# Four GNN layers on one core: phase ends without an all-engine barrier, and semaphores of finished phases cleared by POOL behind a pass's last gather

## What is computed

```python
edge_index = jnp.stack([src, dst])
x = _layernorm(x + _L0_gnn_ref(x, edge_index, ...), axis=-1)                 # attention, exp of clipped dots
x = _layernorm(x + _L1_gnn_ref(x, edge_index, edge_attr_64, ...), axis=-1)   # messages from x[src] and an edge MLP
x = _layernorm(x + _L2_gnn_ref(x, edge_attr_3, edge_weight, src, dst, ...), axis=-1)  # radial MLP, vectors
x = _layernorm(x + _L3_gnn_ref(x, ..., src, dst), axis=-1)                   # softmax over each node's edges
```

## Time and profile before

| | us |
|---|---|
| median of 3 runs (5058.72 to 5064.53) | 5061.64 |
| the profiled execution | 5061.25 |
| its span | 5059.5 |
| mean granted TensorE clock, share of full speed | 0.86 |
| busy: PE, DVE, ACT, POOL | 3558.8, 3631.7, 2794.9, 3588.2 |

### The profile page before, as it was taken

How to read it: one execution, slowest core, us unless ns; L and a number is a source line. 1 busy time by engine, 2 the same in 40 slices (tenths; PEclk the granted TensorE clock), 3 DMA queues, 4 the chain that set the end, 5 groups by cost and what they waited for, 6 DMA issues and landing times. The chain is left out here.

```text
span 5059.5 us, 96093 instructions
## 1 busy us (share of the span) xinstructions
PE 3558.8 (70%) x20064; PEld 2945.0 (58%) x20065; DVE 3631.7 (72%) x8845; ACT 2794.9 (55%) x7180; POOL 3588.2 (71%) x3861
## 2 busy tenths in 40 slices
PE   5445444542476666666688888888779999999993
PEld 4444444442365555555566666666667777777772
DVE  5666666667654444444787777777679999999998
ACT  2444444444622222222576666666558888888885
POOL 4777777775677777776277777777548877777773
PEclk8777777776687777777789999999899999999997
DMA  6544444442433333332022112122157767766662
GB/s 186 157 156 156 156 156 156 156 156 87 122 84 79 80 80 80 80 80 73 28 68 57 56 56 57 56 56 57 38 147 195 191 189 189 190 188 190 189 190 55
DMA packets 491118, 596.80 MB, mean 118 GB/s; under 512 B 127483, under 2 KB 349165, under 8 KB 490639
## 3 DMA queue, kind: packets, MB, share of 16 engines
q0 software_dynamic: 141696, 349.47, 24.9%
q1 hardware_dynamic: 348463, 245.90, 16.9%
q10 hardware_dynamic: 864, 0.39, 0.1%
HBM read 505.89 MB, written 30.07 MB: 106 GB/s over the span
## 5 line engine op out<-in xcount | busy, mean ns | idle before, releaser
L917 DVE TENSOR_TENSOR acc<-acc,banks 128x256 f32 (+1 forms) x3520 | 1346.2, 382 | 599.8 <-PE banks L893 410.1
L893 PE MATMUL banks<-e_rows,e_sel 128*128 128x256 f32 x3520 | 961.2, 409 | 110.4 <-DVE acc L917 105.1
L832 POOL DMA_INDIRECT e_rows<-fsv_t,e_index x820 | 815.7, 995 | 246.9 <-issue 246.9
L832 POOL DMA_INDIRECT e_rows<-kv_t,e_index x820 | 789.9, 963 | 249.7 <-issue 245.5
L832 POOL DMA_INDIRECT e_rows<-x_t,e_index x820 | 774.7, 945 | 257.1 <-issue 243.2
L832 POOL DMA_INDIRECT e_rows<-up_t,e_index x820 | 774.6, 945 | 249.9 <-issue 207.3
L868 ACT ACTIVATE e_away<-node_iota,local 128x128 f32<-128x128 f32 x2640 | 837.0, 387 | 8.4 <-issue 1.9
L893 PEld LDWEIGHTS banks<-e_rows,e_sel 128*128 128x128 f32 x3520 | 663.4, 204 | 253.2 <-DVE acc L917 166.4
L893 PE MATMUL banks<-e_msg,e_sel 128*128 128x137 f32 (+1 forms) x3520 | 756.8, 364 | 7.4 <-DVE acc L917 3.4
L994 PE MATMUL banks<-acc,e_sel_t 128*128 x1760 | 314.4, 334 | 566.9 <-DVE e_sel_t L961 551.9
L1131 ACT ACTIVATE e_rows<-banks,e_rows 128x128 f32<-128x128 f32 x880 | 251.4, 370 | 775.0 <-PE banks L1122 374.0
(11 more groups left out here) (209 smaller groups left out, 6438.0 us busy)
## 6 DMA issues: line engine op xcount, KB each, us to landing
e_near<-near_d SPq DMA_DIRECT2D x440, 258.0 KB, 4.4
e_far<-acc SPq DMA_DIRECT2D x880, 64.0 KB
e_attr<-in_attr_rows SPq DMA_DIRECT2D x880, 32.0 KB
e_rows<-kv_t,e_index POOLq DMA_INDIRECT x820
e_rows<-x_t,e_index POOLq DMA_INDIRECT x820
e_rows<-up_t,e_index POOLq DMA_INDIRECT x820, 2.5
e_rows<-fsv_t,e_index POOLq DMA_INDIRECT x820
kv_t<-proj_kv SPq DMA_DIRECT2D x12, 512.0 KB
```

Of the source, the lines that this page charges most:

```text
L832: G.indirect_dma_start(out=self.rows[:, u, i, 0:self.width], out_offset=None, in_=self.table, in_offset=bass.IndirectOffsetOnAxis(ap=index ...
L893: m = PE.matmul(bank[n_bank][:, col + at:col + at + rows.shape[1]], self.place_of_sel(g)[:, i, :], rows, start=True, stop=True)
L917: V.tensor_tensor(to, to, bank[n_bank][:, col:col + self.sums].unsqueeze(1), ALU.add).then_inc(self.s_added[i], 1)
```

## The change

`Phase.end` no longer has a barrier or clears anything. It puts the phase's semaphores on a list, `earlier`. `EdgePass.run` clears that list on POOL, right behind its own last instruction of the pipeline, with one drain and one range clear for each stretch of neighbouring numbers, and a further drain counts up a new semaphore, `cleared`. Then every engine, instead of SP alone, waits for everything that the pass has still open: the stored tables, the last index load, the clearing and the last addition. Node phases end in the waits that they had. The semaphores of the last phases are not cleared by the kernel.

```diff
     def end(self):
-        self.nc.all_engine_barrier()
-        self.nc.clear_and_free_semaphores(self.sems)
-        self.nc.all_engine_barrier()
+        self.earlier.extend(self.sems)
+
+    def clear_earlier(self):
+
+        self.nc.clear_and_free_semaphores(self.earlier)
+        self.earlier.clear()
...
+    earlier, cleared = [], Counter(nc.alloc_semaphore("cleared"))
...
         def run(self, stages, stored=()):
             pipeline(nc, stages)
-            for sem, count in stored:
-                SP.wait_ge(sem, count)
+
+            self.ctx.clear_earlier()
+            cleared.did(G.drain())
             for e in ENGINES:
+                for sem, count in stored:
+                    e.wait_ge(sem, count)
+                e.wait_ge(self.s_index[0], (N_GROUPS // ROUND - 1) * 16)
+                e.wait_ge(cleared.sem, cleared.at)
                 e.wait_ge(self.s_added[GROUP - 1], N_GROUPS)
-            SP.wait_ge(self.s_index[0], (N_GROUPS // ROUND - 1) * 16)
+                carry(e, self.s_carry)
             self.ctx.end()
```

More of the change, by code:

```diff
@@ L92, with __init__ @@
 class Phase(ExitStack):
-    def __init__(self, nc, tag):
+    def __init__(self, nc, tag, earlier):
         super().__init__()
-        self.nc, self.tag, self.sems = nc, tag, []
+        self.nc, self.tag, self.sems, self.earlier = nc, tag, [], earlier
     def sb(self, name, shape, dt=F32):
@@ L523, in node_phase @@
     def node_phase(tag, make, n_streams=STREAMS, also=None, begin=0.0):
-        with Phase(nc, tag) as ctx:
+        with Phase(nc, tag, earlier) as ctx:
             def blocks(k, steps):
@@ L969, in edges0 @@
     def edges0():
-        with Phase(nc, "e0") as ctx:
+        with Phase(nc, "e0", earlier) as ctx:
             ps = EdgePass(ctx, kv_t, 2 * D, W0)
@@ L1083, in edges1 @@
     def edges1():
-        with Phase(nc, "e1") as ctx:
+        with Phase(nc, "e1", earlier) as ctx:
             w1 = ctx.sb("w1", [ED + 1, D])
@@ L1211, in edges2 @@
     def edges2():
-        with Phase(nc, "e2") as ctx:
+        with Phase(nc, "e2", earlier) as ctx:
             w0 = ctx.sb("w0", [2 * NB, 2 * RH])
@@ L1365, in edges3 @@
     def edges3():
-        with Phase(nc, "e3") as ctx:
+        with Phase(nc, "e3", earlier) as ctx:
             ps = EdgePass(ctx, fsv_t, 2 * D, W3, sels=2, turns=1, cleared=True)
```

## The result

The changed kernel takes 5019.68 us (median; 5018.37 to 5022.47), the kernel before, run beside it, 5063.09 us (5058.72 to 5066.19). The ratio is 0.9915 with a 95% interval of 0.9903 to 0.9927. In the two profiled executions the span falls from 5059.5 to 5018.5 us, by 41.0. Those 41.0 us are what the traces can account for.

What follows compares the result with a forecast made beforehand. It took POOL's gather pace to bound `edges0` to `edges2`, ACT to hold up POOL in `edges3`, and phases to run strictly in sequence. 28.6 + 5.9 + 1.2 - 1.0 = 34.7 us off gave 5027.0 us, range 5022 to 5038.

Steps and rivals of the forecast that it cites:

- Pass ends: Behind the four edge passes: gaps of 30.8 us become 0.8, less 1.4 for late clearing, a gain of 28.6 us.
- late clearing in `edges3`: End of `edges3`: POOL's drain and three range clears end 1.4 us after the last addition, costing 1.4 us.
- Node phases and clock: Barrier pairs removed at node-phase ends and kernel end, 5.9 us, plus 1.2 us from TensorE's clock in `after1`.
- clock term: Start of `after1`: a shorter PE pause gives 2.4 GHz instead of half speed; gain 0 to 1.6 us, taken as 1.2.
- Instruction fetch: Behind `edges3`: DVE's 2.8 us stall, hidden under POOL's drain, comes out; cost 0 to 2.8 us, taken as 1.0.
- Nothing in this change touches the pace: Edge passes: pace stays unchanged, with lengths from first gather to last agreeing within 1 us.
- Rival C: Slower: in one pass a shifted loop needs a fetch each turn, 20 x 2.8 = 56 us, 5083 us; chance 0.03.
- Rival B: After loops: three more fetch stalls of 2.8 us on the path and no clock gain, 5036.6 us; chance 0.07.
- A: Pass ends: drain lasts longer right behind a gather, so clearing in `edges1` ends 2.1 us late, 5029 us; chance 0.07.
- D: Pass ends: the drain's 6.6 us run down only after the pass's rest; only 9.9 us saved, 5051.7 us; chance 0.03.

Runs made afterwards that it cites:

- v7: Kernel before, plus POOL clearing one unused semaphore (increment, clearing DRAIN, range clear) ahead of the barrier at each pass's end; 5041.33 us, ratio 0.9951.
- v8: Changed kernel, plus one plain DRAIN on POOL behind a pass's last gather, ahead of the clearing DRAIN; 5023.59 us, ratio 0.9920 to the kernel before.
- v1: Kernel before, with POOL left out of the wait for a pass's last addition, so its barrier DRAIN follows its last gather; 5036.98 us, ratio 0.9952.
- v2: Kernel before, with one bare DRAIN added on POOL behind each pass's last gather, ahead of the kept wait for the last addition; 5036.63 us, one run.
- v13: Kernel before, with 105 empty DRAINs on DVE near its start and all barriers kept; 5058.36 us, ratio 0.9999.
- v3: Changed kernel, plus one plain DRAIN on POOL behind its end waits of each pass; 5020.12 us, one run.
- v4: Changed kernel, with the whole clearing moved behind POOL's wait for the last addition, onto the path; 5024.54 us, ratio 0.9922 to the kernel before.
- v14: Changed kernel run again, unchanged, beside the kernel before; 5017.47 us, ratio 0.9915.
- v5: Changed kernel, with 30 empty DRAINs on DVE at phase ends, as many as the change took away there; 5035.02 us, ratio 0.9936 to the kernel before.
- v6: Changed kernel, with only the first six padding DRAINs on DVE, at the ends of `project0` and `edges0`; 5028.34 us, one run.

## Why the prediction was wrong, by its own steps

The direction was right and the sum held four fifths of the gain; the time was missed by 7.3 us, and the range by 2.3.

**Pass ends: 28.6 forecast, 29.7 measured.** The 0.2 us a gap was 0.26 (1.05 instead of 0.8 in all), and the number came out near the mark although the path to it was wrong. The 1.4 us of late clearing in `edges3` did not come, because the step before it was wrong: the long drain was called a price of POOL's own for having gathered, paid once, by whatever drain comes next. v7 and v8 show that it is the price of a plain DRAIN; the clearing kind pays 0.1 us. The kernel before could not tell, since there a plain one always came first; both kinds should have been priced, with 0.1 and 6.6 as ends. The prediction also set its 6.59 us against the 12 ns that the Trainium skill (VectorE: DVE Perf Modes, The DRAIN you can't avoid) gives for boilerplate drains. That section speaks of those that the runtime puts ahead of a program and behind it, so the barrier's DRAIN on POOL neither agrees with it nor contradicts it. v8 shows the forecast's world: late by 1.2 - 0.28 = 0.9 us, where 1.4 had been worked out.

**Node phases and clock: 5.9 + 1.2 = 7.1 forecast, about 7.1 measured,** if the medians of the kernels with and without barriers are taken from the table (before, v1, v2, v7, v13 against changed, v3, v4, v8, v14). `project0` gives 2.1 (forecast 2.0), `after0` 3.3 less the 2.2 of its stall, so 1.1 (1.0), `after1` 1.9 (1.0 and 1.2 of clock), `after2` 1.3 (1.0), `after3` 0.7 (0.9). The first pair of traces alone would have misled: it has 0.4 in `after1` and 3.0 in `after2`. The lengths go with the clock: over the whole of `after2` it was 0.94 in the kernel before (88.6 us) and in v4 (88.3 us), and 0.98 in the changed kernel (85.6 us). The granted clock of the changed kernel in stretches of `after1` (first three) and at the start of `after2` (us, PE, PEld, DVE, ACT and POOL busy, clock):

```profile
2387.30:2391.30 4.00, 3.72 (x22) 3.51 (x23) 0.91 (x2) 1.08 (x2) 3.93 (x4) 0.73 0.03 6
2391.30:2395.30 4.00, 1.91 (x12) 1.67 (x11) 4.00 (x5) 1.08 (x2) 3.57 (x3) 0.85 0.00 0
2395.30:2399.30 4.00, 3.96 (x15) 2.82 (x16) 3.31 (x10) 0.60 (x1) 0.00 (x0) 0.58 0.00 0
3617.90:3621.90 4.00, 3.93 (x21) 3.96 (x22) 0.00 (x0) 2.12 (x4) 0.00 (x0) 0.57 0.04 8
```

The full clock forecast for the first 4 us of `after1` was not granted (0.73, against 0.50 in the earlier trace rows), and it fell again soon after (0.85, then 0.58 in the third stretch, PE busy for 3.96 of 4 us). `after2` too started near the 1.2 GHz level, after 2.44 us without PE work. Over all executions the length of `after1` scatters by 3 us within each family, so the clock term of 1.2 us can't be told from scatter, though its sign fits. At that scatter it is in part luck that the 7.1 us agree.

**Instruction fetch: a loss of 1.0 forecast, a gain of some 4.8 measured.** This is the step that failed most, and 5.8 of the missing 7.3 us lie in it. The stall of 2.8 us behind `edges3` was read correctly, and it was expected to come out from under POOL's drain. It does just that in v1, v2 and v7 (gaps of 3.9 to 4.4 us), whose DVE program is unmoved. In the changed kernel it is gone, since 23 instructions fewer stand ahead. The prediction said that the place moves and then still took 1.0 as a loss. And it looked only for stalls that might appear, never for those on the path that might go: 2.2 us in `after0` and 20 times 0.13 us in `edges3`, both in the trace of before. Only the first of these has an instruction packet inside it; the 2.6 us of the loop go with the place as well, but a fetch isn't shown for them. With 4.8 instead of -1.0 and 29.7 instead of 28.6 the sum is 41.6, and the profiled executions differ by 41.0.

**"Nothing in this change touches the pace"** is false for `edges3`. Rival C named the way in part (a loop that starts elsewhere in the program) but priced a turn with a fetch of 2.8 us and only as a loss; the measured size is 0.13 us a turn, with no instruction packet moving, and it was a gain. C's disaster did not occur. Rival B (stalls come out) is what v5 shows in part, though it took 30 padding instructions to bring them back. A (a longer drain right behind a gather) is refuted by v2 and v8, whose drains end 6.6 us behind the last gather. D (the drain only runs down late) is refuted by v1 and v2, whose drains are over before the last addition in three passes.

On fetching, the Trainium skill (Runtime: NRT & Kernel Launch, Instruction fetch mechanics) says that sequential code is prefetched and that a taken branch outside the held window forces a stall. The 2.17 us in `after0` stand in straight code, 28 us and some 100 DVE instructions behind the loop's last branch (1186.9 us), and right behind instructions that had issued without delay; so the trace does not agree that straight code is always covered. The 2.8 us behind `edges3` stand as far behind their loop's last branch (4956.1 us), so no row ties them to a taken branch, which the prediction let them fit.

## What to carry to other kernels

Before costing a barrier on POOL behind gathers, look at which kind of DRAIN comes first there: a plain one was worth 6.6 us, a semaphore clear in front of it removed that for 0.2 to 0.5 us, and a wait on the work itself removes the rest. An edit that changes the number of instructions on an engine can move, take away or bring stalls later on that engine, as it did on DVE here: search the trace of before for idle times ended by nothing, on the path and in each turn of a loop, and give the term a range with both signs instead of one small loss. Read small terms from several executions of a family, since the first pair of traces had two of them off by 1.5 us and more.

## What the runs showed of the hardware that was not expected

- POOL's plain DRAIN behind indirect DMAs takes 6.6 us more, whether it starts ahead of the last gathers (v2, v8), carries a wait or not, or comes 34 us later (kernel before, `edges3`). The DRAIN that belongs to a range clear costs 0.06 to 0.17 us in the same places, and a plain one behind the clear takes 0.03 to 0.05 us (once 0.18, in v7).
- Three stalls of DVE (2.2 us, 2.8 us, 0.13 us in each of 20 turns) were switched by empty DRAINs alone, on in the changed kernel (v5) and off in the kernel before (v13). Packets of the instruction queue moved at the first two and none at the third.
- A loop of `edges3` had three turn lengths with the same work: 55.73 us (before, v1, v2, v5, v7), 55.60 to 55.63 (changed, v3, v4, v6, v8, v14) and 55.53 (v13).
- On one chip every pass took 1.26 to 1.32 times as long in both kernels, with unchanged gaps and node phases, and the change still gained 46 us. What slowed the passes there, no run shows.
